# Moving row norms, routing and root computations to earlier heads in a fused attention and experts kernel

## What is computed

```python
x = x + tanh(g_xattn[1]) * rotary_attention(layernorm(x), ctx, ...)   # 16 heads of 16 features
x = x + tanh(g_ffn[1]) * L1_ffn(layernorm(x), router_W, ...)

def L1_ffn(x):                       # 8 experts, each 256 -> 1024 -> 256
    probs = softmax(x @ router_W + router_b)
    top1 = argmax(probs)             # each row goes to one expert
    h = relu(x @ W1[top1] + b1[top1])
    return probs[top1] * (h @ W2[top1] + b2[top1])
```

## Time and profile before

| what | us |
|---|---|
| median of 3 runs (lowest to highest) | 1344.96 (1342.29 to 1349.06) |
| the profiled execution | 1344.11 |
| its span | 1342.4 |
| beats 0 to 7 of the second block (942.0 to 1130.1) | 188.1 |
| from the last `values` product to the first `up_slot` (1130.1 to 1154.5) | 24.4 |
| from there to the end | 187.9 |

### The profile page before, as it was taken

How to read it: one execution, slowest core, us unless ns; L and a number is a source line. 1 busy time by engine, 2 the same in 40 slices (tenths; PEclk the granted TensorE clock), 3 DMA queues, 4 the chain that set the end, 5 groups by cost and what they waited for, 6 DMA issues and landing times. The chain is left out here.

```text
span 1342.4 us, 27195 instructions
## 1 busy us (share of the span) xinstructions
PE 1171.6 (87%) x8287; PEld 944.8 (70%) x8333; DVE 796.2 (59%) x3047; ACT 624.2 (47%) x1515; POOL 540.8 (40%) x866
## 2 busy tenths in 40 slices
PE   4689999999987999899999999446988877699996
PEld 3466667666654888789999999433656644689995
DVE  4588878888873388865333343176868965423231
ACT  2278787878885233143333333111655544233331
POOL 3334454545433254545333333231544533333331
PEclk9799999999999999899999999866999988799998
DMA  4766675545421971122222222167634884511110
GB/s 107 172 139 167 140 168 112 113 101 115 97 38 20 379 203 33 48 41 37 41 34 40 41 33 36 17 148 167 152 84 116 167 272 152 189 34 48 39 37 5
DMA packets 113526, 136.98 MB, mean 102 GB/s; under 512 B 23115, under 2 KB 99801, under 8 KB 108476
## 3 DMA queue, kind: packets, MB, share of 16 engines
q1 hardware_dynamic: 98152, 106.08, 33.1%
q0 software_dynamic: 15232, 29.17, 9.6%
HBM read 101.85 MB, written 35.97 MB: 103 GB/s over the span
## 5 line engine op out<-in xcount | busy, mean ns | idle before, releaser
L797 DVE CUSTOM_DVE_ANT_0 att_masked_scores<-att_S,Bm 128x256 bf16<-128x256 f32 x512 | 190.3, 418 | 38.2 <-PE att_S L539 26.9
L2459 ACT ACTIVATE moe_hT<-moe_H,moe_b 128x128 f32<-128x128 f32 x312 | 89.0, 368 | 171.5 <-PE moe_H L2372 171.0
L672 ACT ACTIVATE att_PT<-att_T 128x512 f32<-128x512 f32 x256 | 146.2, 591 | 47.6 <-PE att_T L561 43.6
L2384 PE MATMUL moe_Z<-moe_W,moe_hT 128*128 x624 | 141.6, 380 | 0.8 <-DVE moe_z L2684 0.8
L2384 PEld LDWEIGHTS moe_Z<-moe_W,moe_hT 128*128 128x128 f32 x624 | 115.5, 190 | 15.5 <-issue 1.2
L2547 POOL DMA_INDIRECT x<-Y,X x39 | 63.6, 1632 | 154.7 <-DVE Y L2695 150.8
L539 PE MATMUL att_S<-L_KS,L_QS 96*128 96x256 bf16 x512 | 99.3, 276 | 20.3 <-DMA L_KS<-att_k_dram 13.8
L561 PE MATMUL att_T<-L_QS,L_KS 99*128 99x256 bf16 x512 | 97.4, 272 | 11.2 <-ACT att_T L677 3.7
L1825 DVE TENSOR_REDUCE out_mx<-out_S 128x2 f32<-128x512 f32 x128 | 85.4, 685 | 34.5 <-PE out_S L1257 33.4
L2684 DVE TENSOR_TENSOR moe_z<-moe_Z,moe_b 128x256 f32<-128x256 f32 x39 | 16.6, 424 | 141.9 <-PE moe_Z L2384 141.9
L2372 PEld LDWEIGHTS moe_H<-moe_aT,ff_w 128*128 128x128 f32 x832 | 96.8, 192 | 3.1 <-issue 1.9
(11 more groups left out here) (469 smaller groups left out, 2524.2 us busy)
## 6 DMA issues: line engine op xcount, KB each, us to landing
moe_W<-in_L_ffn_W SPq DMA_DIRECT2D x16, 1024.0 KB, 13.7
L_W<-in_L_ffn_W POOLq DMA_DIRECT2D x12, 1024.0 KB, 10.5
att_q_dram<-att_pq SPq DMA_DIRECT2D x16, 384.0 KB, 4.4
att_k_dram<-att_pk SPq DMA_DIRECT2D x16, 384.0 KB, 2.8
L_QS<-att_q_dram SPq DMA_DIRECT2D x16, 384.0 KB, 4.9
L_KS<-att_k_dram SPq DMA_DIRECT2D x16, 384.0 KB, 8.1
L_QS<-att_q_dram SPq DMA_DIRECT2D x16, 256.0 KB, 5.7
L_KS<-att_k_dram SPq DMA_DIRECT2D x16, 256.0 KB, 8.7
```

The costliest lines, as they stand in the source:

```text
L672: nc.scalar.activation(PT[:, h % 8, :], bankT[h % 2][:, :], ACT.Exp).then_inc(exp_done, 1)
L797: ins = nc.vector.tensor_tensor_reduce(masked_scores[:, h % 2, u, :], bankS[h % 2][:, u * SEQ:(u + 1) * SEQ], masks[m // B][0][:, u * SEQ: ...
L2384: ins = nc.tensor.matmul(bankZ[:, 0:D], eT[:, s % 2, f * P:(f + 1) * P], w2e[:, f, :], start=(f == 0), stop=(f == NF - 1))
L2459: ins = nc.scalar.activation(eT[:, s % 2, g * P:(g + 1) * P], bankH[half][:, f * P:(f + 1) * P], ACT.Relu, bias=b1[:, bass.ds(e * NF + g, 1)])
```

## The change

The norm and the routing of each sequence move four to twelve heads ahead, so that beat b holds the whole routing of sequence b - 2, and beat 7 that of sequence 5 with the first slot table.

- `row_stats` of sequence n moves from head 1 of beat n + 2 to head 13 of beat n + 1, right behind `output_rows`; `norm` moves from head 9 to head 0 of beat n + 2, ahead of `queries`. `turn_router`, `logits`, `rank` move to heads 1, 5, 10 of the same beat, with the ACT and DVE steps in heads 3 to 11.
- `early_table` moves into head 11 of beat 7. `row_stats` of sequence 6 is in beat 7 too.
- POOL computes roots at the end of a beat's turn, behind `parts` and `scatter`: first those of sequence b - 1, then the input roots of b + 5. Behind the loop POOL computes no roots any more: those of sequence 6 end its turn in beat 7, and those of sequence 7 are computed on DVE (`quick_roots`, L157, with the number of earlier calls as a new argument).
- Experts 0 to 3 are loaded in beat 5, behind a new wait (`last_stack`) for the last stacked rows. Before, expert 0 was loaded at the end of beat 4, and 1 to 3 in beat 5 without that wait.
- Behind the loop PE turns sequence 6 for the router before `project_out(7)`, and DVE runs `norm(6)` and `expert_matrix(0)` before `output_rows(7)`.

```diff
-def quick_roots(nc, dve, t, q, moments, quick_step, n):
-
-
-    base = QUICK_STEPS * n
+def quick_roots(nc, dve, t, q, moments, quick_step, n, done):
+
+
+    base = QUICK_STEPS * done
...
         return [t for t in LAST_FILL.get(h, ())]
-    more = LAST_BEAT.get(h, ()) if b == B - 1 else ()
     units = [(k, QUADS * b + d if k == "o" else b + d) for k, d in TASKS.get(h, ()) + ROUTE_TASKS.get(h, ())]
-    last = {"o": QUADS * B, "t": EARLY_SEQUENCES1 - 1, "l": EARLY_SEQUENCES1 - 1, "n": EARLY_SEQUENCES1 - 1}
-    return more + tuple((k, n) for k, n in units if 0 <= n < last.get(k, B))
-
-
-ROUTE_TASKS = {1: (("l", -3),), 5: (("n", -3),), 13: (("t", -2),)}
-LAST_BEAT = {11: (("t", 5),), 14: (("l", 5),)}
-DRAIN_TASKS = ("n", 5), ("o", 31), ("a", 7), ("z", 7), ("t", 6), ("l", 6), ("t", 7), ("l", 7), ("n", 6), ("n", 7)
+    last = {"o": QUADS * B, "t": EARLY_SEQUENCES1, "l": EARLY_SEQUENCES1, "n": EARLY_SEQUENCES1}
+    return tuple((k, n) for k, n in units if 0 <= n < last.get(k, B))
+
+
+ROUTE_TASKS = {1: (("t", -2),), 5: (("l", -2),), 10: (("n", -2),)}
+DRAIN_TASKS = ("o", 31), ("a", 7), ("t", 6), ("z", 7), ("l", 6), ("t", 7), ("l", 7), ("n", 6), ("n", 7)
...
                     project_values(2)
-            early = lambda n: 0 <= n < EARLY_ONES - 1
+            early = lambda n: 0 <= n < EARLY_ONES
             for b in range(0, M):
...
                         project_out(b - 1)
-                    if b == M - 1 and h == 11:
-                        turn_router(EARLY_ONES - 1)
                     if h in TURN_AT and 0 <= turning < QUADS * M:
                         turn_out(turning)
-                    if h == 1 and early(b - 3):
-                        logits(b - 3)
-                    if h == 5 and early(b - 3):
-                        rank(b - 3)
-                    if h == 13 and early(b - 2):
+                    if h == 1 and early(b - 2):
                         turn_router(b - 2)
-                    if b == M - 1 and h == 14:
-                        logits(EARLY_ONES - 1)
+                    if h == 5 and early(b - 2):
+                        logits(b - 2)
+                    if h == 10 and early(b - 2):
+                        rank(b - 2)
                     if h in PV_AT and 0 <= quad < QUADS * M:
...
             values(QUADS * M - 1)
-            rank(EARLY_ONES - 1)
             turn_out(QUADS * M - 1)
             turn_heads(M - 1)
+            turn_router(M - 2)
             project_out(M - 1)
-            turn_router(M - 2)
             turn_slot(0)
...
             value_rows(2)
-            early = lambda n: 0 <= n < EARLY_ONES - 1
+            early = lambda n: 0 <= n < EARLY_ONES
             for b in range(0, M):
...
                     quad = QUADS * b + (h - 5) // 4
-                    if h == 6 and early(b - 3):
-                        probabilities(b - 3)
-                    if h == 15 and early(b - 2):
+                    if h == 3 and early(b - 2):
                         bring_router(b - 2)
-                    if b == M - 1 and h == 12:
-                        bring_router(EARLY_ONES - 1)
+                    if h == 8 and early(b - 2):
+                        probabilities(b - 2)
                     if h in PV_AT and 0 <= quad < QUADS * M:
...
             outputs(QUADS * M - 1)
-            probabilities(EARLY_ONES - 1)
             bring_heads(M - 1)
...
+            def last_stack():
+                for side in range(2):
+                    pool.wait_ge(stacked[side][(M - 1) % 3], 16 * N_STACK[side] * ((M - 1) // 3 + 1))
+
             def first_expert():
...
             pool.wait_ge(numbers_made, 2)
+            early = lambda n: 0 <= n < EARLY_ONES
+            input_roots(READY + 1)
             for b in range(0, M):
-                if has(b + 4):
-                    input_roots(b + 4)
+                if b == 7:
+                    stacked_expert(5, M - 2)
                 if has(b + 3):
                     parts(b + 3, 0)
-                if b == 7:
-                    stacked_expert(5, M - 2)
-                if has(b - 2):
-                    inverse_roots(nc, pool, t, moments, root_step, b - 2).then_inc(rooted, 1)
-                if has(b + 3):
                     parts(b + 3, 1)
                     keep_values(b + 3)
-                if b == 4:
+                if b == 5:
+                    last_stack()
                     first_expert()
-                if b == 5:
                     second_expert()
...
                     stacked_expert(4, M - 3)
-                if b == 3:
+                if b == 2:
                     pool.wait_ge(none_in, 16)
-                if 0 <= b - 3 < EARLY_ONES - 1:
-                    scatter(b - 3)
-            scatter(EARLY_ONES - 1)
-            inverse_roots(nc, pool, t, moments, root_step, M - 2).then_inc(rooted, 1)
+                if early(b - 2):
+                    scatter(b - 2)
+                if has(b - 1):
+                    inverse_roots(nc, pool, t, moments, root_step, b - 1).then_inc(rooted, 1)
+                if has(b + 5):
+                    input_roots(b + 5)
             rows_in(0)
-            inverse_roots(nc, pool, t, moments, root_step, M - 1).then_inc(rooted, 1)
             for s in range(1, EARLY):
...
                 else:
-                    quick_roots(nc, dve, t0, quick, moments0, quick_step, n)
+                    quick_roots(nc, dve, t0, quick, moments0, quick_step, n, n)
                 normal_rows(nc, here(X, n), here(Y, n), t0).then_inc(x_normed, 1)
...
             def norm(m):
-                dve.wait_ge(rooted, m + 1)
+                if m < M - 1:
+                    dve.wait_ge(rooted, m + 1)
+                else:
+                    quick_roots(nc, dve, t, quick, moments, quick_step, m, READY + 1)
                 normal_rows(nc, here(X, m), here(Y, m), t).then_inc(normed, 1)
...
                     input_moments(4)
-            early = lambda n: 0 <= n < EARLY_ONES - 1
+            early = lambda n: 0 <= n < EARLY_ONES
             for b in range(0, M):
...
                     turning = QUADS * b + (h - 7) // 4
+                    if h == 0 and has(b - 2):
+                        norm(b - 2)
                     if h == 0 and has(b + 3):
                         queries(b + 3)
-                    if h == 1 and has(b - 2):
-                        row_stats(b - 2)
-                    if h == 2 and has(b + 4):
+                    if h == 3 and has(b + 4):
                         input_norm(b + 4)
...
                         turned_keys(b + 3)
+                    if h == 6 and early(b - 2):
+                        top_expert(b - 2)
+                        centre(b - 2)
                     if h == 7 and has(b + 1):
...
                         max_columns(b + 1)
-                    if h == 9 and has(b - 2):
-                        norm(b - 2)
+                    if h == 11 and early(b - 2):
+                        destinations(b - 2)
+                        expert_weights(b - 2)
+                    if b == M - 1 and h == 11:
+                        early_table()
                     if h == 12 and has(b - 1):
                         output_rows(b - 1)
+                    if h == 13 and has(b - 1):
+                        row_stats(b - 1)
                     if b == 0 and h == 6:
...
                         input_moments(b + 5)
-                    if h == 2 and early(b - 3):
-                        top_expert(b - 3)
-                        centre(b - 3)
-                    if h == 6 and early(b - 3):
-                        destinations(b - 3)
-                    if h == 10 and early(b - 3):
-                        expert_weights(b - 3)
-                    if b == M - 1 and h == 15:
-                        top_expert(EARLY_ONES - 1)
-                        centre(EARLY_ONES - 1)
                     if h in TURN_AT and 0 <= turning < QUADS * M:
                         normalise(turning)
-            row_stats(M - 2)
-            destinations(EARLY_ONES - 1)
             normalise(QUADS * M - 1)
-            expert_weights(EARLY_ONES - 1)
-            early_table()
+            norm(M - 2)
+            expert_matrix(0)
             output_rows(M - 1)
-            norm(M - 2)
             row_stats(M - 1)
-            expert_matrix(0)
             norm(M - 1)
```

## The result

The changed kernel takes 1355.12 us (median of 7 runs, 1350.42 to 1356.76) against 1344.96 for the kernel before (7 runs beside it, 1342.29 to 1349.06). The ratio is 1.0064, with a 95% interval from 1.0044 to 1.0083: slower by about 0.6%. The forecast was 1343.5, with a range up to 1353: the measured time lies above both. The profiled execution has a span of 1353.4 us, 11.0 more than before.

The account below looks back on a forecast made before the run. It took PE's waits in beats 2 and 5 and behind beat 7 as the bound, PE and DVE nearly full in beats 3 and 4. -10.3 + 4.4 + 2.1 + 4.1 + 2.2 - 6.1 + 2.1 = -1.5: median 1343.5, range 1330 to 1353.

Parts of the forecast that it names:

- step 3: Beats 1 to 4: added routing, late parts and DVE waits cost +2.2 us, with bounds -5 and +9.
- Rival B: Beats 1 to 3: POOL's two root chains and DVE's head 0 wait go through in full; 1353, chance 0.17.
- Step 1: Beat 5: the gate on the expert loads removes the stacked-rows wait and the slow clock behind it, -10.3 us.
- Step 2: Beats 5, 6, 7: with norm at head 0, PE waits at `turn_router`; +4.4, +2.1, +4.1 us.
- Step 4: Behind beat 7: a shorter path from the last `values` to `up_slot`, V + 18.3 for V + 24.4, -6.1 us.
- Step 5: The clock behind the three new waits in beats 5 to 7: 0.7 us each, +2.1 us.
- Rival A: The waits at head 0 don't appear or are short; about 1328, or 1336 with half of them; chance 0.30.
- Rival C: Beat 5: the gate does nothing, the key stack still lands 17 us into the beat; 1349, chance 0.05.

Follow-up runs that it names:

- e1: The changed kernel with ACT's `bring_router` moved from head 3 to the start of head 2, ahead of `first_part` of the queries: 1346.03 us.
- e4: The kernel before with only the gate: experts 0 to 3 loaded in beat 5 behind the wait for the last stacked rows: 1340.33 us.
- e6: The changed kernel without the gate: expert 0 loaded at the end of beat 4, 1 to 3 in beat 5, no stack wait: 1357.73 us.
- e3: The changed kernel with `norm` at head 2, `turn_router` at head 3, `bring_router` at head 4, and `logits` and `top_expert` one head later: 1344.89 us.
- e10: The kernel of e3 with `input_norm` on DVE also moved from head 3 to head 6: 1338.31 us.
- e5: The changed kernel with POOL's two root chains ahead of the query parts of beats 2 and 3 joined into one: 1351.69 us.
- e7: The changed kernel with the edits of e1 and e5 together: 1355.25 us.
- e2: The changed kernel with POOL's input roots between query parts and key parts of the next beat, and `input_norm` at head 5: 1370.85 us.

## Why the prediction was wrong

**The step that failed is step 3, beats 1 to 4: +2.2 forecast.** Measured at the exponentials, beat 1 changed by -0.2 and beats 2, 3, 4 by +4.6, +7.4 and +1.7: +13.5 for the step. The miss on the median is 11.6 us, and this step alone is off by 11.3. The working had the late parts (POOL's two chains; forecast 7.8 us from the moments to the parts, measured 7.7: 1015.68 to 1023.36) and DVE's wait at head 0 (0.7 forecast in beats 2 and 3 and 1.7 in beat 4; 0.75 and 1.67 measured). It followed the lateness only to `first_part` of the keys. It overlooked that the change itself puts `bring_router` behind `first_part` of the queries on ACT, and `turn_router` into the list two places ahead of `keys`. So a late part on POOL holds PE in head 4, through a bank that has nothing to do with it. e1 shows this: with that one order turned round, 12.4 us of it are gone. The bound of +9 that I gave the step was too narrow as well, because it held each delay in full but not the clock behind them.

**Rival B was the nearest.** It named the two chains, ACT behind `first_part`, the clock, and 1353. Its sign (beats 2 to 4 over 87 us) came: 93.8. But its mechanism went by DVE's waits that are never got back. DVE's wait at head 0 was 0.75 us, and e1 kept it (0.73) and still had its 8 us; what cost was the bank. I gave it 0.17. It priced that at 1353, and even so came short.

**Step 1, the gate, -10.3: half of the size.** In beat 5 of the kernel before it is worth 4.8 (e4). I read the 8.3 us of key_off as its own time from issue to landing. But it lands with the two stacks ahead of it, after 10.3 us in e4 and 11.8 in the changed kernel, which is 14.0 us into beat 5 and not 11. Nor did the slow clock behind the wait, which I had counted at 2.9, go in e4. In the changed kernel the gate is worth nothing in beat 5 (e6). Forecast for beat 5 were 23, measured 24.8.

**Step 2, norm at head 0: mechanism right, two sizes off.** The waits for Y came in all three beats, at 3.11, 3.13 and 2.25 us instead of 4.4 to 4.7. They came in beats 2 to 4 too, 1.54 us each, which the sum had nowhere. At the turn to beat 6 the chain took 7.8 us from the end of `project_out` (1099.25) to that of the norm (7.4 forecast), but PE had 4.7 us to fill it with, not 2.7. DVE's rows there, to be set beside the earlier trace rows:

```profile
1100.02 0.75 DVE L1857 SCALAR_TENSOR_TENSOR X<-out_z,gates,X 128x512 f32<-128x512 f32 x1
1102.07 0.25 DVE L118 BATCH_NORM_AGGREGATE out_mv<-out_stats 128x2 f32<-128x6 f32 x2
1106.27 0.74 DVE L183 TENSOR_SCALAR Y<-X,out_mv,out_r 128x256 f32<-128x256 f32 x2 [1.68 <-POOL out_r L141]
```

Yet beat 6 grew by 6.0 and not 2.1. The 2.3 us that it should have got back did not come: the wait of 1.44 us is gone, but the beat has 1.20 us for `out_MQ` instead, and 1.80 us before beat 7 for turned maxima. Beat 7 came out right, +4.4 for 4.1, but by luck: its wait for Y is half of the forecast, and PE is busy for 2.2 us more (16.68 for 14.50), where I had 1.0 less work and no more than 0.7 for the clock. Its 2.07 us wait at `turn_out(30)` behind the table is the 2.1 of the working:

```profile
1147.38 0.41 PE L1304 MATMUL out_A<-ident,out_OTS 128*128 128x128 f32 x2 [2.07 <-DVE out_AO L1847]
```

e3 and e10 confirm the mechanism: with norm two heads later beat 6 gives back 3.7 and 3.9 us, and the part from there to the first `up_slot` 4.0 and 3.7.

**Step 4, behind beat 7, -6.1: right, slightly better.** 17.0 us measured for 18.3. The rows in order: norm of 6 after 2.77 us of waiting, `project_out(7)` 3.61 us at the low clock, the gather only 1.37 late, the last norm at 1163.80.

**Step 5, the clock, +2.1: too small.** After waits of 3.1 us the values product ran in 1.93 instead of 1.07 us, and PE's busy time in beat 6 grew by 1.7 (17.47 for 15.78, with two products fewer). The 0.7 per wait was the middle between two rows, and the outcome is not in the middle: behind the waits shown here the clock either held or was slow for some us. The full 1.5 that I had by the rule of the Trainium skill (TensorE: Matmul & The Clock Gate, Part 1) was nearer. The clock cost most where the sum had no term for it: behind the keys wait of beat 3, an estimated 4.8.

**Rival A** is excluded by the waits of 3.11, 3.13 and 2.25 us; its line was 2. **Rival C** is half right. The stack landed 14.0 us into beat 5, not 17, beat 5 is 3.8 us shorter, and in the kernel before the gate does bring 4.8 (e4). But that the gate does nothing for beat 5 of the changed kernel is what e6 measured.

## What to carry to other kernels

When an instruction is moved to another place on an in-order engine, list what stands right ahead of it there and what that waits for; then list who takes over the buffer that it empties. The lateness of an engine three steps away came out on PE through such a shared bank, and most of it was cured by a single exchange: reader of the bank first, late input second. Joining two chains, or moving one, did not help here, because the joint chain had to wait for the later moments (e5, e7), and the moved one held up its reader on DVE (e2).
